# Two token blocks through one feed-forward stage: the second block's gate and up products side by side with the first's

## The reference

```python
w = weights[subjects]; y = einsum('bct,bcd->bdt', x, w)       # mix: a 64x64 matrix chosen per sample
gu = y @ ternary(w_gate_up).T; gate, up = split(gu)           # 512 -> 2 x 2048
h = silu(gate) * up
x = x + rms_norm(h) @ ternary(w_proj).T                       # 2048 -> 512
z = x @ W.T + (x @ A_b.T) @ B_b.T * scaling                   # per-sample rank-16 adapter
logits = z @ router_w.T + router_b                            # 8 experts for each of 512 outputs
c = top-2 softmax weights, summed over the outputs
x = x + sum_e c[:, e] * (z @ expert_w[e].T + expert_b[e])
```

## Time and profile before

| | |
|---|---|
| median of 3 runs | 2214.53 us (2214.19 to 2214.58) |
| the profiled execution | 2214.39 us |
| its span, first to last instruction | 2212.7 us |
| mean granted TensorE clock | 0.999 |
| TensorE busy | 2192.0 us, 99% |
| VectorE busy | 1627.9 us, 74% |
| ScalarE busy | 1053.4 us, 48% |
| GpSimd busy | 60.3 us, 3% |

### The profile page before, as it was taken

How to read it: one execution, slowest core, us unless ns; L and a number is a source line. 1 busy time by engine, 2 the same in 40 slices (tenths; PEclk the granted TensorE clock), 3 DMA queues, 4 the chain that set the end, 5 groups by cost and what they waited for, 6 DMA issues and landing times.

```text
span 2212.7 us, 28732 instructions
## 1 busy us (share of the span) xinstructions
PE 2192.0 (99%) x9809; PEld 1809.1 (82%) x9817; DVE 1627.9 (74%) x2119; ACT 1053.4 (48%) x1493; POOL 60.3 (3%) x55
## 2 busy tenths in 40 slices
PE   7999999999999999999999999999999999999999
PEld 5778888888888888888888888888888888888887
DVE  8986444444444445689999999999898888888883
ACT  7764333333323233588777878777332222222221
POOL 0000000101010002000000000000000000000000
PEclk9999999999999999999999999999999999999999
DMA  6313303242424223412212121116222222222120
GB/s 210 105 53 126 98 20 107 81 111 76 112 77 113 89 61 139 158 70 81 81 71 85 71 85 71 62 67 262 104 100 85 81 85 81 94 71 100 66 85 24
DMA packets 157908, 205.66 MB, mean 93 GB/s; under 512 B 63330, under 2 KB 96674, under 8 KB 155682
## 3 DMA queue, kind: packets, MB, share of 16 engines
q1 hardware_dynamic: 114578, 149.95, 20.4%
q10 hardware_dynamic: 43152, 55.06, 7.5%
q0 software_dynamic: 128, 0.07, 0.0%
HBM read 136.35 MB, written 68.68 MB: 93 GB/s over the span
## 4 chain that ended last, share of the span: by engine, by line
PE 93%; issue 4%; DVE 2%; ACT 1%; POOL 1%; ACTq 0%; POOLq 0%; DVEq 0%
PE slot L1656 18%; PE ex_bank L1833 10%; PE ex_bank L1831 10%; PE ex_bank L1832 10%; PE pj L1669 9%; PE high_bank L1800 5%; PE high_bank L1798 5%; PE high_bank L1802 5%; PE low_bank L1800 4%; PE low_bank L1798 4%; PE low_bank L1802 4%; PE slot L1718 3%; PE slot L1625 1%; PE slot L1707 1%; PE ex_bank L1846 1%
## 5 line engine op out<-in xcount | busy, mean ns | idle before, releaser
L1656 PE MATMUL slot<-y_hi,wgu 128*128 128x512 f32 x1024 | 402.4, 393 | 1.3 <-ACT wgu L767 0.7
L1656 PE MATMUL slot<-y_lo,wgu 128*128 128x512 f32 x1024 | 399.6, 390 | 0.0
L1831 PE MATMUL ex_bank<-ew_hi,hb 128*128 128x512 f32 x992 | 385.9, 389 | 0.0
L1833 PE MATMUL ex_bank<-ew_lo,hb 128*128 128x512 f32 x992 | 385.9, 389 | 0.0
L1832 PE MATMUL ex_bank<-ew_hi,hb 128*128 128x512 f32 x992 | 385.9, 389 | 0.0
L1103 ACT ACTIVATE ex_bank<-eb_sb 128x512 f32<-128x512 f32 x248 | 149.3, 602 | 451.1 <-DVE acc L1562 391.5
L1512 DVE SCALAR_TENSOR_TENSOR lead_in<-code_in,wts 128x1024 bf16<-128x1024 bf16 x256 | 311.7, 1218 | 7.5 <-ACT wts L1043 5.8
L1656 PEld LDWEIGHTS slot<-y_hi,wgu 128*128 128x128 f32 x1024 | 192.8, 188 | 45.2 <-DVE q_scale L1173 2.9
L1656 PEld LDWEIGHTS slot<-y_lo,wgu 128*128 128x128 f32 x1024 | 192.8, 188 | 39.7
L1831 PEld LDWEIGHTS ex_bank<-ew_hi,hb 128*128 128x128 f32 x992 | 186.2, 188 | 38.7
L1833 PEld LDWEIGHTS ex_bank<-ew_lo,hb 128*128 128x128 f32 x992 | 186.2, 188 | 38.7
(11 more groups left out here) (169 smaller groups left out, 3494.3 us busy)
## 6 DMA issues: line engine op xcount, KB each, us to landing
hb<-h_scratch SPq DMA_DIRECT2D x34, 512.0 KB, 3.3
code_scratch<-half_code SPq DMA_DIRECT2D x32, 512.0 KB, 2.6
half_in<-code_scratch SPq DMA_DIRECT2D x32, 512.0 KB, 3.3
hb<-h_scratch ACTq DMA_DIRECT2D x30, 512.0 KB, 3.6
h_scratch<-ht ACTq DMA_DIRECT2D x48, 256.0 KB, 2.9
q_raw<-in_w_ffn SPq DMA_DIRECT2D x21, 512.0 KB, 3.4
x_scratch<-x_res ACTq DMA_DIRECT2D x8, 1024.0 KB, 4.5
lead_scratch<-lead SPq DMA_DIRECT2D x32, 256.0 KB, 2.0
```

Of the source, the lines that this page charges most:

```text
L1656: last = mm(slot[s % 2][:, g, :], wgu[:, c, r * P:(r + 1) * P], y[:, c, :], start=(c == 0 and v == 0), stop=(c == DC - 1 and v == 1))
L1831: mm(ex[e][:, :], hb[:, u, c, 0, :], ew_hi[:, e, c, :], start=False, stop=False, skip_group_check=True)
L1833: last = mm(ex[e][:, :], hb[:, u, c, 0, :], ew_lo[:, e, c, :], start=False, stop=(c == DC - 1), skip_group_check=True)
```

## The change

- The list FIRST, and with it the order of TensorE, has gu(1,j) right behind gu(0,j), and gu(1,j+1) behind gu(0,j+1). Nothing of gu is left after squares(0), whose slot use is now the last of FIRST.
- The mix of block 1 (second_mix) runs right after mix(0), before quant(2), and writes into the four projection banks, which hold nothing yet. It has semaphores of its own.
- SP gathers four of the block 1 weights before it loads raw weights, POOL the other four behind its first four.
- On ScalarE silu(1,j) stands behind quant_out(3h+2) and square(0,j); before, silu(1,j-2) stood between quant_out(3h+1) and quant_out(3h+2). 
- The banks of slots and projection swap once: uses of FIRST and proj(0,..) have slot_first and pj_first, all later ones slot and pj, which lie in the other's banks. proj(1,0) may so start before the residual of block 0 has read its sums; it waits for the slots to be drained. The projection's four parts run in the order 3, 2, 1, 0.
- second_hidden is taken apart into highs, squares and lows. Of VectorE's order, lows 1 and 2 move ahead of the residual; the split of the small and linear weights stays behind the adds of squares and ahead of low 4.
- turn(0,u) comes at p = 3, 4 (before: 1, 2), adapt at 8 (5), linear at 10 and 13 (7 and 10); on the other two engines correspondingly.
- The router's and experts' bank lists are turned by four.

```diff
-GU_ORDER = []
+GU_ORDER = [(i, j) for j in range(HC) for i in range(2)]
 for _h in range(PAIRS):
     _j = 2 * _h
...
+    FIRST += [f"gu{_j}@0", f"gu{_j}@1"]
     FIRST += [f"q{k}" for k in quant_of(_h)[:2]]
...
+    FIRST += [f"gu{_j + 1}@0", f"gu{_j + 1}@1"]
     FIRST += [f"q{k}" for k in quant_of(_h)[2:]]
-SECOND = ["ss"] + [f"gu{_j}" for _j in range(HC - AHEAD, HC)] + ["t0", "t1", "xa", "h0", "h1"]
+FIRST.append("ss")
+SECOND = ["t0", "t1", "xa", "h0", "h1"]
...
 def second_ring(p):
-    return 1 if p == HC - 1 else p % 4
+    return (p + 2) % 4
 def second_freed(p):
...
+    return HC - 3 + p
...
+        slot_first = [pb(f"slot_first{s}", [P, 2, BLK], pfirst) for s in range(2)]
+        pj_first = pb("pj_first", [P, SUB, D], pfirst)
+        pfirst.close()
+        pj = pb("pj", [P, SUB, D], pa)
         slot = [pb(f"slot{s}", [P, 2, BLK], pa) for s in range(2)]
...
-        plane = high_bank + low_bank[:3]
+        plane = low_bank + high_bank[:3]
...
-        ex = [ex_bank[s] for s in (3, 4, 5, 6, 7, 0, 1, 2)]
+        ex = [ex_bank[s] for s in (7, 0, 1, 2, 3, 4, 5, 6)]
...
+        def bank(n, s):
+            return (slot_first if isinstance(n, int) and n < len(FIRST) else slot)[s % 2]
...
-            gather_mix(1, mixw1, mixw1_in, range(3))
+            gather_mix(1, mixw1, mixw1_in, range(SPB // 2))
             load_raw(3)
             load_raw(4)
-            gather_mix(1, mixw1, mixw1_in, range(3, SPB))
...
+            pool.wait_ge(dconst, 2)
+            for q in range(SPB // 2, SPB):
+                v = pool.value_load(subject_i[0:1, SPB + q:SPB + q + 1], min_val=0, max_val=E - 1)
+                r = (q % 2) * C
+                pool.dma_start(mixw1[r:r + C, q // 2, r:r + C], cond_w[bass.ds(v * C, C), :]).then_inc(mixw1b_in, 16)
...
# ScalarE
             mix(0)
             quant_in(2)
+            second_mix()
             quant_in(3)
...
                 silu(0, j)
                 quant_out(3 * h + 1)
-                if h:
-                    silu(1, j - 2)
                 quant_out(3 * h + 2)
                 act.wait_ge(drained, use(0, f"gu{j}")[0] + 1)
                 square(0, j, hid[:, j % 2, :])
+                silu(1, j)
...
+            for p in range(3):
+                second_high(p)
+            second_square(0)
+            second_high(3)
+            second_square(1)
+            second_square(2)
             store_x1(0)
             small_weights()
             linear_weights()
+            second_square(3)
             for p in range(4, HC):
-                second_hidden(p)
+                second_high(p)
+                second_square(p)
...
+            store_h(0, 1)
...
# VectorE
             squares(0, HC - 1)
-            finish(0)
-            second_hidden(0)
-            second_product(HC - 2)
-            for p in range(1, 4):
-                second_hidden(p)
-            second_product(HC - 1)
+            second_low(0)
+            variance(0)
+            second_low(1)
+            second_low(2)
+            residual(0)
+            squares(1, 0)
+            second_low(3)
+            squares(1, 1)
+            squares(1, 2)
             small_weights()
             linear_weights()
+            squares(1, 3)
             for p in range(4, HC):
-                second_hidden(p)
+                second_low(p)
+                squares(1, p)
...
# TensorE
+            def second_mix():
+                pe.wait_ge(xmix1_in, 16)
+                pe.wait_ge(mixw1_in, 8 * SPB)
+                pe.wait_ge(mixw1b_in, 8 * SPB)
+                for c in range(DC):
+                    for k in range(SUB):
+                        last = mm(pj_first[:, c, k * P:(k + 1) * P], x_res[:, k, c * P:(c + 1) * P], mixw1[:, k, :],
+                                  start=True, stop=True)
+                    if c % 2:
+                        last.then_inc(mix1_filled, 1)
...
-                if j == 0 and not first_block(i):
+                if j == 0 and first_block(i):
+                    pe.wait_ge(mix1_drained, 2)
+                elif j == 0 and second:
+                    pe.wait_ge(drained, use(1, f"gu{HC - 1}")[0] + 1)
+                elif j == 0:
                     pe.wait_ge(x1_ready, i * SUB)
-                for k in range(SUB):
+                for k in reversed(range(SUB)):
+                    if j == 0 and second and k == 0:
+                        pe.wait_ge(drained, use(1, "ss")[0] + 1)
...
             mix(0)
+            second_mix()
             quant(2)
             for h in range(PAIRS):
                 gu(0, j)
-                if h:
-                    gu(1, j - 2)
+                gu(1, j)
...
                 gu(0, j + 1)
-                if h:
-                    gu(1, j - 1)
-                else:
-                    mix(1)
+                gu(1, j + 1)
...
             squares(0)
-            for j in range(HC - AHEAD, HC):
-                gu(1, j)
             for p in range(HC - 1):
                 proj(1, p, SECOND_ORDER[p])
-                if p in (1, 2):
-                    turn(0, p - 1)
-                if p == 5:
+                if p in (3, 4):
+                    turn(0, p - 3)
+                if p == 8:
                     adapt(0)
-                if p == 7:
+                if p == 10:
                     linear(0, 0)
-                if p == 10:
+                if p == 13:
                     linear(0, 1)
```

More of the change, by code:

```diff
@@ L745, in mix @@
                     act.wait_ge(filled, n + 1)
-                    nc.scalar.activation(y[:, 2 * u:2 * u + 2, :], slot[s % 2][:, :, :], ACT.Copy)\
+                    nc.scalar.activation(y_hi[:, 2 * u:2 * u + 2, :], bank(n, s)[:, :, :], ACT.Copy)\
+                        .then_inc(act_half, 1)
+            def second_mix():
+                for u in range(2):
+                    act.wait_ge(mix1_filled, u + 1)
+                    nc.scalar.activation(y1_hi[:, 2 * u:2 * u + 2, :], pj_first[:, 2 * u:2 * u + 2, :], ACT.Copy)\
                         .then_inc(act_half, 1)
@@ L1161, in mix @@
             def mix(i):
-                hi, lo = (y1_hi, y1_lo) if isinstance(i, int) and i == 1 else (y_hi, y_lo)
                 for u in range(2):
@@ L1165, in mix, with second_mix @@
                     dve.wait_ge(act_half, act_halves(i, u) + 1)
-                    nc.vector.tensor_tensor(lo[:, 2 * u:2 * u + 2, :], slot[s % 2][:, :, :],
-                                            hi[:, 2 * u:2 * u + 2, :].bitcast(F32), ALU.subtract).then_inc(drained, 1)
+                    nc.vector.tensor_tensor(y_lo[:, 2 * u:2 * u + 2, :], bank(n, s)[:, :, :],
+                                            y_hi[:, 2 * u:2 * u + 2, :].bitcast(F32), ALU.subtract).then_inc(drained, 1)
+            def second_mix():
+                for u in range(2):
+                    dve.wait_ge(act_half, act_halves(1, u) + 1)
+                    nc.vector.tensor_tensor(y1_lo[:, 2 * u:2 * u + 2, :], pj_first[:, 2 * u:2 * u + 2, :],
+                                            y1_hi[:, 2 * u:2 * u + 2, :].bitcast(F32), ALU.subtract).then_inc(mix1_drained, 1)
             def quant_scale(k):
@@ L1222, in second_product @@
                     dve.wait_ge(hid1_out[j % RING], 16 * (j // RING))
-                nc.vector.tensor_tensor(hid1[:, j % RING, :], gate[:, gu_count(1, j) % 2, :], slot[s % 2][:, 1, :],
+                nc.vector.tensor_tensor(hid1[:, j % RING, :], gate[:, gu_count(1, j) % 2, :], bank(n, s)[:, 1, :],
                                         ALU.mult).then_inc(drained, 1)
@@ L1267, in finish, with residual @@
                     dve.wait_ge(inv_ready, i)
-                nc.vector.tensor_scalar(var[:, :], slot[s % 2][:, 0, 0:SUB], 1.0 / HID, EPS, ALU.mult, ALU.add).then_inc(drained, 1)
+                nc.vector.tensor_scalar(var[:, :], bank(n, s)[:, 0, 0:SUB], 1.0 / HID, EPS, ALU.mult, ALU.add).then_inc(drained, 1)
+            def residual(i):
+                sums = pj_first if isinstance(i, int) and i == 0 else pj
                 dve.wait_ge(inv_ready, i + 1)
@@ L1677, in squares @@
                 for k in range(SUB):
-                    last = mm(slot[s % 2][:, 0, k:k + 1], sumsq[:, k * P:(k + 1) * P], ones_col[:, :], start=True, stop=True)
+                    last = mm(bank(n, s)[:, 0, k:k + 1], sumsq[:, k * P:(k + 1) * P], ones_col[:, :], start=True, stop=True)
                 last.then_inc(filled, 1)
@@ L1693, in turn @@
                     for k in range(SUB):
-                        last = nc.tensor.transpose(slot[s % 2][:, b, k * P:(k + 1) * P],
+                        last = nc.tensor.transpose(bank(n, s)[:, b, k * P:(k + 1) * P],
                                                    x_res[:, k, c * P:(c + 1) * P], ident[:, :])
@@ L1706, in adapt @@
                 for q, (w, y, c) in enumerate(prods):
-                    last = mm(slot[s % 2][:, 0, :], w[:, c, :], y[:, c, :], start=(q == 0), stop=(q == len(prods) - 1))
```

(3 more changed lines are left out.)

153 lines of the change are left out of this document (64 added, 89 removed).

## The result

The changed kernel takes 2219.58 us (median of 11 runs, 2218.23 to 2222.84) beside 2214.46 for the one before (11 runs, 2211.98 to 2215.64). The ratio of the two is 1.0025, with a 95% interval of 1.0017 to 1.0032. So it is slower by 5.1 us. The forecast was 2217.2, 2.7 us slower, with "within 0.2%" as the likely verdict; the measured time is just inside the upper end of the range, 2219.6, but 0.23% to 0.25% slower is more than was called likely. The profiled run took 2220.18 with a span of 2218.5.

A forecast was written before the change was run, and what follows sets the result against it. TensorE, busy 2192.0 of 2212.7 us, bounds the kernel, so only its idle or half-clock time can change. Terms -3.2 + 1.0 + 4.75 + 1.9 - 1.86 + 0.15 = +2.7 gave 2217.2 us, range 2212.5 to 2219.6.

The forecast's parts named there:

- Part 1: Start of the kernel: the second mix right after mix(0) fills TensorE's idle and avoids the half clock; gain 3.2 us.
- Rival 3: Start: POOL's gathers late by 2 us or more, the gain becomes about 0, 2220.4 us; chance 0.08.
- Part 2: Steady pairs h = 1 to 6: silu behind quant_out and square comes 0.17 later a pair; 1.0 us lost.
- Part 3: End of FIRST: TensorE waits for VectorE before block 1's fifth projection, 4.75 us, with clock loss and removed waits after it.
- Both waits of before: Tail of block 1: waits before the adapter product and last-but-one projection go; gain 1.86 us.
- The half clock: After the wait at block 1's fifth projection: TensorE runs at 1.2 GHz, charged 1.9 us (0 to 1.9).
- 0.15: End of block 1: store_h(0,1) keeps ScalarE, so mix(2)'s y_hi is late at gu(2,0); 0.15 us lost.
- the late fetch: Block 1 tail: SP's hidden-chunk fetches 5 to 9 land about 202.7, projection 10 due at 203.5; cost 0 to 0.6.
- Number 2: Start: new waits at 28.4 to 31.3 bring a second half-clock stretch, +1.9 us, 2219.1; chance 0.14.
- Rival 4: End of FIRST: the fifth low is not late, only gains stay, 2210.5 us; chance 0.06.

The follow-up runs named there:

- e1: Changed kernel with silu(1,j) moved back ahead of quant_out(3h+2) and square(0,j) on ScalarE; 2214.66 us.
- e2: Changed kernel with silu(1,j) placed between quant_out(3h+2) and square(0,j); 2215.57 us.
- e3: Kernel before the change with silu(1,j-2) moved behind quant_out(3h+2) and square(0,j); 2217.61 us.
- e4: Changed kernel with the small and linear weights' split moved behind p = 5 and SP's fetches 5 to 9 ahead of the x_mix load; 2218.05 us.
- e5: Changed kernel with 16 additional matmuls in TensorE's wait before the fifth projection of block 1; 2218.53 us.
- e7: e6 with the linear weights in four quarters behind p = 4, 5, 6 and 9, and the fifth high and low one step earlier; 2208.87 us.
- e8: e5 with SP's fetches 5 to 9 of the hidden chunks ahead of the x_mix load and its gathers; 2217.41 us.
- e9: Changed kernel with only SP's fetches 5 to 9 moved ahead of the x_mix load and its gathers; 2219.66 us.
- e10: Changed kernel with all eight block 1 gathers on SP and none on POOL; 2224.28 us.
- e6: Changed kernel with silu(1,j) first as in e1, linear weights and fetches as in e4, small weights split in the last pair; 2211.31 us.

## Why the prediction was right and wrong

**Part 1, the start: right.** Second mix at 16.86 (16.5 forecast), quant(4) behind a wait of 1.61 (1.8), gu(0,1) at 31.83 (31.3) behind 0.53 (0.65), all with the releasers that were named. The gain is 2.9 by the table (3.2 forecast). The forecast counted the half clock of the kernel before, 1.9 us, as there in every run; by the mean clocks above it seems to be missing in 28 of 75. POOL's four gathers kept their step: they begin at 8.34, 9.48, 10.63 and 11.77, 0.52 long each, the first three beside VectorE's tensor_tensor instructions. The Trainium skill, SBUF — State Buffer, section "Who interferes with whom", excepts these from the lock on descriptors; the trace agrees, with 1.14 to 1.15 us from one to the next as in the kernel before. Rival 3 did not happen.

**Part 2, the pairs: the mechanism right in kind, its size wrong, and this is the step that failed.** The forecast had silu(1,j) at 103.65 instead of 103.47, 0.17 later a pair, 1.0 us in all. Measured: 0.5 a pair, 3.0 us over the six. The working let the square start when its product was drained and ScalarE free. But square(0,j) also waits for ss_ready, VectorE's add of square j-1, because there is one sq buffer, and that add stands behind product(0,j). Its row is there: the add at 108.56, the square at 109.34, where quant_out's start at 108.08 and the 0.95 that such a pass costs its successor would have let it start at 109.03. The same wait was counted in Part 3 and left out here. Before the change it was harmless, since silu did not stand behind it. The trace of the kernel before had the row for it, in VectorE's timeline:

```profile
102.67 0.68 DVE L1248 TENSOR_TENSOR sumsq<-sumsq,sq 128x512 f32<-128x512 f32 x1
```

With 0.78 from the add's start to the square's (108.56 to 109.34) and 0.54 from the square to silu (109.34 to 109.88), silu would have come at 103.99 instead of 103.47, 0.52 late, close to the measured 0.5. This is reckoned afterwards, with the two steps taken from the changed kernel. Of the delay, 0.31 (109.34 less 109.03) is the wait for the add, 1.9 us over six pairs; the other 0.2 is the 0.17 that the forecast had. So the order of the instructions was read rightly, and the term was short by the wait. e1, e2 and e3 show that the place of silu does all of it, in either kernel.

**Part 3, the wait: right.** 4.95 us before the fifth projection (4.75 forecast, lower bound 3.9), released by a y_lo difference of VectorE. e4 shows by its 1.17 that the place of the weights' split decides. Both waits of before (1.86) went. **The half clock: right in kind, a little short in size**: 2.6 us in the profile (projection 3.78 against 1.81, turning 1.51 against 0.87) and 1.5 to 2.3 by experiments, where 1.9 was forecast. The tail as a whole lost 5.6 where the sum had 4.75 + 1.9 - 1.86 + 0.15 = 4.9; the 0.2 of the wait and the 0.7 of the half clock are most of the rest. The half clock also covered the late fetch. The forecast had that at 0 to 0.6; it cost nothing in the changed kernel, and a wait of 1.30 once the clock was kept (e5).

**The rivals.** Number 2 (a half clock after the waits at the start) was given 0.14. The profile of the changed kernel doesn't show it, three of the four others with the same start do. It should have had about a half. The miss doesn't hang on it: the profile without it is 5.8 us slower than that of before. The Trainium skill, TensorE: Matmul & The Clock Gate, "What's actually happening", has the number of cold (half-clock) matmuls at a kernel's start vary from run to run of the same kernel; these profiles, of kernels that are the same up to there, agree: 7.56 us in two of them and 9.17 or 8.62 in three, for the same two gu's behind the same wait.

**The sum.** Forecast +2.7; by the profile +5.7 at block 2 (by the medians +5.1). Of the 3.0 between them, 2.0 is the pairs, 0.7 the tail, and 0.3 the start. Rival 4, the faster outcome, failed where it was said to, on VectorE's program order. With the pairs at their measured 3.0 the sum would have been +4.7, over the 4.4 that "within 0.2%" allows; that verdict was lost mainly by one uncounted semaphore.

## What to carry to other kernels

When an instruction moves behind another on an in-order engine, take over all the waits of the one in front, one by one: a wait that cost nothing becomes a wait of everything that now stands behind it. When work is taken out from between two stages because TensorE has something better to do earlier, ask what it covered: here the two products hid some 5 us of VectorE work, and the early start paid only when that work was itself spread over later stages (e7, 5.5 us faster than before). Two waits in a row can hide each other, so one should remove or fill both before a price is put on either.

## What the runs showed of the hardware

Behind the same kind of wait near 28 to 32 us, 2.7 us with 0.6 of work in it, TensorE's granted clock fell to half in three profiles (e4, e8, e9) and not in two (the changed kernel's, e5), nor behind the same wait in e10, with 1.1 to 1.6 us between them. mix(0), behind other work, took 5.44 us at half clock in e1 and e6 and 3.8 in the ten other profiles. So a profile of one execution shows whether a half clock can fall behind a short wait, and not how often. Behind an idle of 4.8 to 4.95 us it fell in each profile that has one (the changed kernel, e1, e2, e9, e10), and with 3.9 us of otherwise useless matmuls in that idle it did not fall (e5, e8). The price was 1.5 to 2.3 us between profiles with and without it. Shorter idles brought it too: 2.15 us in the kernel before, 2.50 in e4.
